# Cross attention: row sums for eight and four key tiles at a time, with GpSimd keeping a running total

## What is computed

```
def _mha(x, y, wq, wk, wv, li1_w, li1_b, ...):          # B = 16, 256 queries, 1601 keys, H = 16 heads, D = 32
    xn = _ln(x, lnx_g, lnx_b)
    yn = _ln(y, lny_g, lny_b)
    q = jnp.einsum('bsc,hcd->bhsd', xn, wq)
    k = jnp.einsum('btc,hcd->bhtd', yn, wk)
    v = jnp.einsum('btc,hcd->bhtd', yn, wv)
    a = jax.nn.softmax(jnp.einsum('bhsd,bhtd->bhst', q, k) * D ** (-0.5), axis=-1)
    ...
    o = jnp.einsum('bhst,bhtd->bhsd', a, v)
```

## Time and profile before

| | |
|---|---|
| median of 3 runs | 7573.08 us (7554.94 to 7580.55) |
| the profiled execution's own time | 7585.29 us |
| its span, first to last instruction | 7583.5 us |
| mean granted PE clock | 0.944 |
| stage `cross` (first exponential to last) | 3908.6 to 5738.4 us, 16 batches of about 115.2 us |
| PE busy, 4000 to 4500 us | 485.62 of 500 us |
| POOL busy, 4000 to 4500 us | 296.19 of 500 us |

### The profile page before, as it was taken

One profiled execution on the slowest core, in us unless ns is written; L12 is line 12 of the kernel. 1 busy time (PEld: TensorE's weight loads), 2 busy tenths in 40 slices (PEclk: granted clock), 3 DMA queues, 4 the chain that ended last, 5 costly groups with the idle time before them and its releaser, 6 DMA issues. The chain is left out here.

```text
span 7583.5 us, 186164 instructions
## 1 busy us (share of the span) xinstructions
PE 6919.7 (91%) x73814; PEld 3121.0 (41%) x73814; DVE 5700.1 (75%) x12751; ACT 4999.8 (66%) x9974; POOL 2322.2 (31%) x2368
## 2 busy tenths in 40 slices
PE   7999999977999999789769999999996899999979
PEld 3333333344333333344434445445454433333335
DVE  6888888855989898677657677776764389998955
ACT  4777777753888888356446666666663178888842
POOL 2222222111121211055435555565554021212100
PEclk9999999987999999889979999999998599999989
DMA  4334333302343433100100000000002134344300
GB/s 93 87 87 92 82 87 87 84 25 68 83 97 79 100 75 69 34 17 21 40 24 10 9 8 11 6 10 9 5 5 56 48 86 96 87 89 94 78 26 12
DMA packets 318292, 412.95 MB, mean 54 GB/s; under 512 B 56437, under 2 KB 237957, under 8 KB 317432
## 3 DMA queue, kind: packets, MB, share of 16 engines
q1 hardware_dynamic: 308818, 395.82, 22.8%
q10 hardware_dynamic: 8614, 5.21, 0.3%
HBM read 225.41 MB, written 174.66 MB: 53 GB/s over the span
## 5 line engine op out<-in xcount | busy, mean ns | idle before, releaser
L691 ACT ACTIVATE a_probs<-scores_ps 128x512 f32<-128x512 f32 (+2 forms) x5248 | 2820.7, 591 | 367.7 <-PE scores_ps L611 276.2
L750 DVE TENSOR_REDUCE a_unit_max<-bank 128x1 f32<-128x512 f32 x3072 | 2003.8, 683 | 202.6 <-PE bank L598 168.0
L628 PE MATMUL bank<-a_probs,a_v_sb 128*9 128x256 f32 (+1 forms) x20992 | 1634.8, 384 | 29.2 <-ACT a_out_sb L698 20.2
L1302 ACT ACTIVATE cross_probs<-scores_ps 128x512 f32<-128x512 f32 (+1 forms) x1792 | 869.0, 570 | 549.3 <-PE scores_ps L1196 549.3
L1386 DVE TENSOR_REDUCE cross_unit_max<-bank 128x1 f32<-128x512 f32 x1536 | 981.2, 685 | 292.7 <-PE bank L1182 289.6
L611 PE MATMUL scores_ps<-a_stack 49*128 49x256 bf16 (+1 forms) x10496 | 1147.7, 277 | 56.1 <-ACT a_probs L691 54.9
L750 DVE TENSOR_REDUCE a_unit_max<-scores_ps 128x1 f32<-128x512 f32 x1536 | 1049.8, 683 | 150.7 <-PE scores_ps L598 133.5
L598 PE MATMUL bank<-a_stack 48*128 48x512 bf16 (+2 forms) x3413 | 1053.2, 377 | 7.3 <-DMA a_stack<-a_stack_dram 2.0
L1467 POOL TENSOR_TENSOR cross_added<-cross_probs 128x1024 f32<-128x1024 f32 x384 | 906.6, 2361 | 274.8 <-PE bank L1229 193.8
L611 PEld LDWEIGHTS scores_ps<-a_stack 49*128 49x128 bf16 (+1 forms) x10496 | 377.2, 96 | 1000.7 <-ACT a_probs L691 830.8
L515 POOL CAST a_parts<-a_qk 128x512 bf16<-128x512 f32 (+3 forms) x225 | 118.0, 524 | 1930.6 <-ACT a_qk L710 1831.9
(11 more groups left out here) (420 smaller groups left out, 9909.9 us busy)
## 6 DMA issues: line engine op xcount, KB each, us to landing
a_stack_dram<-a_parts SPq DMA_DIRECT2D x288, 400.2 KB, 4.2
a_stack<-a_stack_dram SPq DMA_DIRECT2D x256, 348.2 KB, 8.0
a_stack<-a_stack_dram SPq DMA_DIRECT2D x128, 444.2 KB, 10.0
a_ctxT<-in_ctxT SPq DMA_DIRECT2D x48, 400.2 KB, 4.9
a_stack_dram<-a_parts SPq DMA_DIRECT2D x288, 64.0 KB, 2.4
a_stack_dram<-a_parts SPq DMA_DIRECT2D x96, 128.0 KB, 2.4
f_x<-x_after_dram SPq DMA_DIRECT2D x32, 256.0 KB, 3.2
x_after_dram<-a_res SPq DMA_DIRECT2D x48, 128.0 KB, 4.5
```

What stands on the lines that cost most here:

```text
L628: ins = pe.matmul(out_bank[32 * h:32 * h + V8, q0:TOK], v[0:n, e.t, 4 * e.g + h, :], A.probs[0:n, held, o + q0:o + TOK], start=(e.t == 0), ...
L691: act.activation(by_pair(A.probs[0:n, b, a * 512:(a + 1) * 512])[:, :, q0:TOK], by_pair(score_bank[(2 * e.i + a) % 3][0:n, :])[:, :, q0:TO ...
L750: ins = dve.tensor_reduce(unit_max[:, e.g % 2, qt, 2 * a + j, c:c + 1], bank[:, 0:e.s.chunks[c][1]], AX.X, ALU.max)
L1302: act.activation(probs[0:n, b, h, 0:m, :].rearrange("p m q -> p (m q)"), score_bank[h][0:n, 0:m * TOK], ACT.Exp, scale=scale).then_inc(S[" ...
```

## The change

The ones matmuls are made three times a quad in place of seven: for the sum of eight tiles (j = 0 to 3), of four tiles (j = 4 and 5), and for the single last one. POOL adds up each such lot in one slot of `added`. The pair that opens a lot (j = 0, 4) is one add of two tiles as before; each pair that joins (j = 1, 2, 3, 5) is two adds onto the slot, one for each tile, each behind a wait for POOL's own add before it. PE counts `pv` with a new semaphore, and ACT, before it writes a `probs` buffer again, waits for that buffer's `pv` and for POOL's adds out of it. A slot of `added` is written again when the `sums` of the lot two lots ago are done. With `own` set the instructions stay as they were.

```diff
+    def is_pair(self, j):
+        return self.pairs[j][1] - self.pairs[j][0] == 2
+
+    def joins(self, j):
+        return not self.own and j in (1, 2, 3, 5)
+
+    def sums_at(self, j):
+        return self.own or j in (3, 5, 6)
...
         if pv:
-            plan.append(Ev("sums", s=s, g=steps[k][0], j=steps[k][1], i=zero + k))
+            if s.sums_at(steps[k][1]):
+                plan.append(Ev("sums", s=s, g=steps[k][0], j=steps[k][1], i=zero + k))
...
+            e.mixed, e.multiplied = mixed.get(e.i - BUFS32), multiplied.get(e.i - BUFS32)
+        if e.kind == "mix" and s.is_pair(e.j):
+            e.done = adds
+            adds += 2 if s.joins(e.j) else 1
+            mixed[e.i] = adds
+            if s.joins(e.j):
+                added[e.i] = adds
+                added.pop(e.i - 1)
+            else:
+                lots += 1
+                added[e.i] = adds
+            lot_of[e.i], e.lot = lots - 1, lots - 1
+            e.free = None if s.joins(e.j) else lot_summed.get(lots - 1 - ADDS32)
...
-                        both = added[0:n, e.i % ADDS32, h, :] if t1 - t0 == 2 else probs[0:n, e.i % BUFS32, h, 0, :]
+                        both = added[0:n, e.lot % ADDS32, h, :] if t1 - t0 == 2 else probs[0:n, e.i % BUFS32, h, 0, :]
...
+                    if not own and e.multiplied:
+                        act.wait_ge(S["pv"], e.multiplied)
+                    if not own and e.mixed:
+                        act.wait_ge(S["added"], e.mixed)
...
-                    pool.tensor_tensor(added[:, e.i % ADDS32, :, :], probs[:, b, :, 0, :], probs[:, b, :, 1, :],
-                                       ALU.add).then_inc(S["added"], 1)
+                    total = added[:, e.lot % ADDS32, :, :]
+                    if s.joins(e.j):
+                        for m in range(2):
+                            pool.wait_ge(S["added"], e.done + m)
+                            pool.tensor_tensor(total, total, probs[:, b, :, m, :], ALU.add).then_inc(S["added"], 1)
+                    else:
+                        pool.tensor_tensor(total, probs[:, b, :, 0, :], probs[:, b, :, 1, :], ALU.add).then_inc(S["added"], 1)
```

More of the change, by code:

```diff
@@ L977, in schedule32 @@
     side, cast, rows, summed, added = {}, {}, {}, {}, {}
+    adds, lots, lot_of, lot_summed, mixed, multiplied = 0, 0, {}, {}, {}, {}
     for e in plan:
@@ L1013, in schedule32 @@
             e.free = summed.get(e.i - BUFS32)
[L1014 to L1017, removed]
+            e.mixed, e.multiplied = mixed.get(e.i - BUFS32), multiplied.get(e.i - BUFS32)
[11 more added lines that the diff above has]
+            e.free = None if s.joins(e.j) else lot_summed.get(lots - 1 - ADDS32)
         if e.kind == "pv":
+            multiplied[e.i] = len(multiplied) + 1
             e.takes = takes if e.j == 0 else 0
@@ L1022, in schedule32 @@
             e.added = added.get(e.i)
+            if e.added:
+                e.lot = lot_of[e.i]
+                lot_summed[e.lot] = summed[e.i]
         if e.kind == "take":
@@ L1077, in heads32 @@
                                   "side_done", "cast", "max_scores0", "max_scores1", "max_scores2", "max_taken", "max_rows", "scores0",
-                                  "scores1", "scores2", "scores3", "probs", "added", "kept", "sums", "normed", "logs", "inverse",
+                                  "scores1", "scores2", "scores3", "probs", "added", "pv", "kept", "sums", "normed", "logs", "inverse",
                                   "x_out", "dve_own", "ln_minus", "ln_shift"] + LN_SEMS)
@@ L1219, in program_pe @@
                             else:
-                                pe.matmul(out[:, 0:TOK], v[0:n, t, cols], probs[0:n, b, h, m, :], start=opens, stop=False,
-                                          skip_group_check=True)
+                                ins = pe.matmul(out[:, 0:TOK], v[0:n, t, cols], probs[0:n, b, h, m, :], start=opens, stop=False,
+                                                skip_group_check=True)
+                    if not own:
+                        ins.then_inc(S["pv"], 1)
                 if e.kind == "sums":
```

## The result

The kernel became slower by a third of a per cent. The median of 20 runs is 7595.72 us (7575.72 to 7625.34), and 7569.93 us (7554.94 to 7580.64) for the kernel before in 20 runs beside them: ratio 1.0036, interval 1.0027 to 1.0044. The forecast was 7586 us with 7545 to 7626 around it. The profiled execution took 7611.67 us, 16 us above its own median; that of before took 7585.29 us, 15 us above.

A forecast was written before the change was run, and what follows sets the result against it. PE bounds the kernel before; after the change POOL's chain to the q cast was to make PE wait. +8 us from the quads and +5 us from the shared port, on 7573, gave 7586 us, range 7545 to 7626.

The forecast's parts named there:

- POOL's chain: From k cast through six dependent joining adds to q cast: ends at 21.98 us, PE's first unit starting at 22.11.
- A: First of a batch's four quads, lettered in order, each cut at k's second-part cast; forecast 28.51 us, 29.02 before.
- C: Third quad of a batch, where the layer norm falls on POOL; forecast 30.63 us, 30.07 before.
- the loss of the sums' saving: The saving of the sums in steps 2 to 4 is lost whole, since POOL is late next.
- would stand and wait for POOL in every quad: PE's first unit in step 6 waits for the q cast 1 to 2 us a quad, some 60 to 100 us.
- PE has let DVE catch up while it stood: PE's second unit in step 6 no longer waits 0.66 us for a bank; unit to next k cast is 6.40 us.
- the fewer matmuls leave PE's clock as it is: PE stands still one to two us a quad, and its granted clock was assumed unchanged, at no cost.
- the three others are worth 1.71 us a quad at most: Groups of sums removed from steps 2, 3 and 4 save PE at most 1.71 us a quad.
- PE stays the bound: Rival: PE still sets the pace and keeps 1.71 us a quad, 109 us in all, giving 7464 us; chance 0.07.
- The port: DVE's additions at L1411 and POOL's adds block each other; costs POOL about 0.3 us a batch, +5 us.
- DVE is shut out in C: Rival: both L1411 additions wait a whole POOL add each, +24 us, giving 7610 us; chance 0.15.
- The rivals on the gap: Between dependent POOL adds: no bubble, 7537 us, chance 0.08; or a bubble twice as long, 7621 us, chance 0.20.

The follow-up runs named there:

- 6: Changed kernel with the bf16 copy of q made by ACT in place of POOL's cast, all ten adds a quad kept: 7565.71 us, ratio 0.9993.
- 11: Changed kernel with the lots of 10, (0, 1), (2), (3, 4), (5), (6), and q's cast on POOL: 7722.47 us, ratio 1.0186.
- 5: Kernel before with four more POOL adds a quad, as in 4, without DVE's two output-bias additions in this stage: 7588.18 us, ratio 1.0025.
- 3: Changed kernel with one add in place of two for each joining pair, its second tile left out of the sum: 7556.6 us, ratio 0.9977.
- 1: Changed kernel with the projection and cast of q three steps earlier, step 2 of a quad in place of step 5: 7584.22 us, ratio 1.002.
- 4: Kernel before, all seven groups of sums kept, with four more POOL adds a quad into a spare tile: 7638.27 us, ratio 1.0085.
- 2: Changed kernel with lots of four tiles only: nine adds a quad for ten, three groups of sums gone for four: 7568.12 us, ratio 0.9993.
- 7: On top of 6, PE makes the second tile's value products behind the k or v job, not ahead of it: 7562.91 us, ratio 0.9995.
- 8: Kernel before with ACT's two new waits alone, and PE's new count of pv: 7571.21 us, ratio 1.0.
- 10: On top of 6, other lots: (0, 1), (2), (3, 4), (5), (6), eight adds a quad: 7535.66 us, ratio 0.9953.
- 9: On top of 6, DVE's copies out of the max bank cut to 128 columns, rest of second k and v tiles left out: 7552.14 us, ratio 0.9969.

## Why the prediction was right or wrong

**Right: POOL's chain.** The gaps between dependent adds are 0.08 us where the add has one new wait and 0.14 where it has two (0.08 and 0.15 in the sum), the six joining adds take 14.66 us in the median, and the q cast ends within 0.02 us of the forecast in A. C came out at 30.63 us to the hundredth, D at 27.93 for 28.04. Experiments 6 and 11 show that this date, and not POOL's load, is what costs: with ten adds and no date for the cast the stage is 8 us shorter than before (6), and with eight adds and a later date it is 117 us longer than that of the changed kernel (11).

**Right: the loss of the sums' saving.** Experiment 5 agrees that the four groups gain next to nothing while POOL is late. But there was little to lose: 0.19 us a quad with POOL out of the way (3), not 1.71.

**Wrong: PE "would stand and wait for POOL in every quad", 60 to 100 us.** It was 27 us in 27 places of 55, in B and D. The reason is in the point on the 1.71 us below: PE gained so little in steps 2 to 4 that in A and C it came no earlier than POOL: with POOL out of the way (3) it is at the unit at 21.90, 20.24, 22.00 and 21.16 us in A, B, C and D, for 22.09, 20.82, 21.98 and 21.15 before. The length of C was right all the same, since POOL's chain sets it together with PE.

**Mis-sized: quad A,** 28.83 for 28.51 us. "PE has let DVE catch up while it stood" held in B, where the unit to the next k cast took 6.46 us (forecast 6.40), but not in A, where PE arrived at nearly the same time as the cast: 6.82 us there. Experiment 6 shows A's own length without POOL: 28.83 us too. The term was worth 0.3 us a batch, 5 us in all.

**Wrong: "the fewer matmuls leave PE's clock as it is".** The clock fell in three quads of the profiled execution. They are 31.15 to 31.38 us long for 28.45, about 2.8 us each, 8.4 us together. The text had seen that PE would stand one to two us in every quad and asked the rows of before about it, which hold no stall of that length. In experiments 1 and 6, without the stall, no clock fell; in 4, with a wait of 2.0 us in C, it fell in 13 batches, and in 11, with one of up to 1.8 us in nearly every quad, 44 times. In 5, where PE waits 1.2 us for the cast in B, it didn't fall until the last batch. One short fall in the last batch stands in 2, 3, 7, 8 and 10 too, and so the two of the changed kernel there can't be put down to the cast. The wider spread of the changed kernel's runs (50 us for 26) would fit falls that some executions have more of; that is argued, since each has but one profile.

**Wrong: "the three others are worth 1.71 us a quad at most", as a value.** As a bound it stands, but the rival *PE stays the bound* took it whole and gave 7464 us. Experiment 3 measured 0.19 us a quad. PE was busy 97% of a quad and yet its next limit was a few tenths away in every step: DVE's copy out of the bank (a wait of 0.6 us) in the steps with k and v; in the others PE's list shows short waits on ACT's exponentials and on the turned row (11.6 and 3.2 us in 1600), and what ends each of those steps was not tested. The sums filled the gap of the copies: B's step without a copy got shorter (3), the others did so when the copy was cut (9), and the group of step 5, with no copy beside it, was worth 0.41 to 0.57 us (10). It cost the forecast nothing, since POOL was taken as the bound, but all of my expectations for experiments 1 to 3 went wrong by it.

**The port.** The +5 us can't be found in the changed kernel: in the usual batch one of the two additions takes 1.51 us before and about 1.68 in the changed kernel, the other 0.28 us in both, and C is as forecast without the term. The median of 892 in the earlier trace rows, on which the text leaned, is the middle between these two lengths. The rival *DVE is shut out in C* is real and larger than its 24 us, but in another kernel: in 4, where the adds fall otherwise, it cost 48 us. There the second addition lost to POOL's next add as well. The order in time decided, and the trace of before doesn't show how it would fall.

**The sum.** Against +13 us there are +26 in the medians. The starts of the casts of k's second part, quad by quad in both kernels, add up: 8.7 us for the 54 windows in the middle of the stage (0.66 us a batch, forecast 0.51), 8.4 us for the clock in three of them, 1.5 us for the first quad (32.48 for 30.99), 3.2 us for the last seven windows and 4.5 us from the last cast to the end of the stage. So the term that the text had in its sum was sized well, and two thirds of the +26 lie in terms that it had at nothing: the clock and the two ends of the stage. The port's +5, which did not come, made up for a part of them. That the median is only 10 us from the forecast is luck to that extent.

**The rivals on the gap** are settled: no bubble-free adds, no doubled gap. ACT's new waits cost nothing that shows, as said (8).

## What to carry to other kernels

Before work is taken off the busiest engine, ask in each step what else ends in the time that it filled, and take out the part that covers nothing: two groups of sums gave 34 us of the stage (10), four had given 8 to 10 (6 and 3). Work given to a slack engine with a strict order is priced by the dates of what stands behind it (here a cast of 0.40 us), so move the dated item away first. And count a new stall of PE of one to two us dearer than its length, since its clock may fall with it: a quad with a fall was 2.8 us longer than one with the same stall alone.

## What the runs showed of the hardware

- TensorE's clock fell to the 1.2 GHz level within 2.0 us behind a stall of 1.40 us, in three quads where PE was busy over 90% of the time, and 16 matmuls then took 1.94 us for 1.07. In the other quads B the same stall was followed by no fall. The Trainium skill (TensorE: Matmul & The Clock Gate, Part 1: The HAM clock gate) ties the lower level to an idle or cold engine; the trace agrees on the two levels, and here stalls of 1.40 us (changed kernel) and 2.01 us (4) stood ahead of the falls.
- A DVE addition with both inputs in SBUF, 278 ns when alone, took up to 2452 ns beside GpSimd's back-to-back adds. The Trainium skill (SBUF — State Buffer, Who interferes with whom) says that such an instruction and a GpSimd instruction that reads SBUF block each other for the whole instruction; experiment 4 agrees, and shows that two in a row can each lose (4.16 us); in the kernel before only the first did (1.51 and 0.28 us).
- GpSimd adds of 128x1024 in f32 follow each other at 2.44 us with one semaphore wait between them and at 2.50 us with two, 2.36 us of it the add.
